# Self-attention scores in three single PSUM banks with one exponential per head, and a shared ring of four banks in place of five

## The chip, the cores and the metric

The kernel runs on one NeuronCore of one Trainium2 chip. The metric is the time of one execution on the device in microseconds (us). PE is the matrix engine, PEld its weight loads, DVE the vector engine, ACT the scalar (activation) engine, POOL is GpSimd, SP issues the DMAs. PSUM, where PE writes its results, has eight banks; a bank holds 512 float32 numbers on each of 128 partitions.

## The reference

Four layers run over `x` of shape 4 x 1024 x 256 (batch, tokens, features), all in float32:

```python
# L0: block with adaLN, rotary positions, a self mask, cross attention over 77 context tokens, MLP
x = x + g_msa * (attn(q, k, v, mask) @ attn_out_W)
x = x + g_x * (attn(qc, kc, vc) @ co_W)
x = x + g_mlp * (gelu(xm @ mlp_W1 + mlp_b1) @ mlp_W2 + mlp_b2)
# L1: prototypes, a router and three experts, gated; no self attention
# L2: the same shape of block as L0, self attention without mask or rotary positions
# L3: a second cross attention over the context
def attn(q, k, v):
    s = einsum('bhqd,bhkd->bhqk', q, k) * scale      # 16 heads of width 16
    return einsum('bhqk,bhkd->bhqd', softmax(s), v)
```

The change concerns the self attention of L0 and L2 directly, and everything else of L0, L2 and L3 through the PSUM banks. In L0 only 256 of the 1024 keys count for the inputs given (the path called `few`).

## The kernel before, in words

The program is written by engine, in the five blocks `@block.sync`, `.tensor`, `.vector`, `.scalar` and `.gpsimd`, with semaphores between them. L1 has banks of its own choice. L0 is one `Region` (`FEWR`), L2 and L3 are another (`L2R`). A region has one list of tokens, `R.order`, which a planner (`overlapped`) writes from estimated costs and due times; every engine walks the same list and does its part of each token. The planner isn't touched, so the order is the same before and after.

The tokens: `lnT` turns normalised rows (two banks), `qk` and `v` are the projections, `slot` is a piece of self attention, `oT`/`oP` the output projection, `cq`, `cm`, `cn`, `cs`, `cp`, `ct` are the six steps of cross attention, `m1`/`m2` the MLP. `cm` computes scores to find their maxima, and takes four banks at once; DVE reduces them one by one (L1564). `cn` turns the maxima into a row, which DVE adds into the queries in two updates (L1570). `cs` computes four score tiles, one bank each, which ACT exponentiates (L1743). `cp` is the product with the values, copied out by ACT (L1680), and `ct` turns the result back. For one half of a batch's queries `cross_tokens` writes `cm[0], cm[1], cm[2], cn[0], cm[3], cs[0], cn[1], cp[0], cs[1], ct[0], ...`; the planner puts tokens of other streams between them.

A slot has scores for 128 keys x 512 queries of four heads (one key tile), and beside them "fills", score tiles for a later group whose row maxima DVE takes (L1424, in L0 L1422), and the product of the slot before. PE does it in two halves:

```python
for half in range(2):
    if score is not None:
        scores(score, half)
    for key in R.fills(fills, half):
        fill(key)
    if half == 0 and product is not None:
        pv(product)
```

`scores(t, half)` makes two heads, `fill` one tile, two fills a half; the four matmuls sit in four 32-row groups of the array and run side by side. `pv(t)` makes four products into the accumulator bank 7. There are 64 slots with scores in L0 and 256 in L2; each region begins with slots that have fills alone.

The banks: 0 and 1 belong to the scores. A half writes both, one ACTIVATE (L1701) reads both, 1024 columns, into `PB` and counts `R.ex` up; the next half waits for that count. Banks 2 to 6 are the ring: every other result of a region takes the next one in turn (`take`), whoever makes it, after waiting that the reader of the key five before it has counted `ring_free` up. Bank 7 is the accumulator. All matmuls go through the helper at L814; transposes have lines of their own (L960 `oT` tails, L971, L980 `lnT`/`oT`, L1078 `cn`, L1100 `ct`). PE's instructions are issued in order, so a wait in one holds up all behind it.

Of the kernel before, what the change touches and what calls it, by code (L numbers as in the profile page):

```python
# [11 lines left out]
ACT = mybir.ActivationFunctionType  # L12
AX = mybir.AxisListType

P = 128
# [4 lines left out]
HG = 4  # L20
NG = H // HG
HALF = 512
# [39 lines left out]
def pixart_kernel(nc, io):  # L62
    ctx = ExitStack()
    with ctx:
# [183 lines left out]

        RING = (2, 3, 4, 5, 6)
        ACC = 7  # L250

        class Region:
# [3 lines left out]
            def __init__(self, name, l, few, overlap):  # L256
# [19 lines left out]
                n = 0  # L276
                for tok in self.order:
# [9 lines left out]
                    for add in self.bias_adds(tok):  # L287
                        self.adds[add] = len(self.adds)
                self.ring_full, self.ring_free = (sems(name + side, "0 1 2 3 4") for side in ("ring_full", "ring_free"))
                self.s_full, self.ex, self.pv, self.acc, self.nm, self.rec, self.crec = sems(name, "scores_T_full exp_done pv_done acc_out max_done recip cross_recip")  # L290
# [68 lines left out]
            def closing(self):  # L359

                return sorted(self.number, key=self.number.get)[-5:]

            def bank(self, key):
                return RING[self.number[key] % 5]

            def full(self, key):
                return self.ring_full[self.number[key] % 5], self.number[key] // 5 + 1

            def freed(self, key):
                return self.ring_free[self.number[key] % 5], self.number[key] // 5 + 1  # L370

            def fills_up(self, key):
                return self.ring_full[self.number[key] % 5]

            def frees(self, key):
                return self.ring_free[self.number[key] % 5]

# [434 lines left out]
        def _(pe):  # L812
# [69 lines left out]
            def region_pe(R):  # L882
                def take(key):
                    n = R.number[key]
                    if n >= 5:
                        pe.wait_ge(R.ring_free[n % 5], n // 5)
                    return RING[n % 5]

# [25 lines left out]
                def scores(t, half):  # L914
                    b, g, qh, i = R.at(t)
                    kt = R.keys[i]
                    pair = 2 * t + half
                    if pair:
                        pe.wait_ge(R.ex, pair)
                    if half == 0 and i == 0:  # L920
                        pe.wait_ge(*R.freed(("nm", b * NG + g, qh)))
                    for j in (2 * half, 2 * half + 1):
                        rows = slice(32 * j, 32 * j + 32)
                        last = mm(PS[:, j % 2, :], KE[rows, g, kt * P:(kt + 1) * P], QE[rows, g, qh * HALF:(qh + 1) * HALF], True, not R.masked)
                        if R.masked:
                            for q in range(4):
                                last = mm(PS[:, j % 2, q * P:(q + 1) * P], MQ[:, qh * 4 + q, kt * P:(kt + 1) * P], bigI[:, :], False, q == 3)
                    last.then_inc(R.s_full, 1)

                def pv(t):  # L930
                    b, g, qh, i = R.at(t)
                    pe.wait_ge(R.ex, 2 * t + 2)
                    if i == 0:
# [744 lines left out]
        def _(act):  # L1678
# [9 lines left out]
            def region_act(R):  # L1688
# [5 lines left out]
                def slot(tok):  # L1694
                    _, score, fills, product, tails, nms = tok
                    if score is not None:
                        for half in range(2):
                            act.wait_ge(R.s_full, 2 * score + half + 1)
                            if half == 0 and score >= 2:
                                act.wait_ge(R.pv, score - 1)  # L1700
                            act.activation(PB[:, score % 2, 2 * half:2 * half + 2, :], PS[:, 0:2, :], ACT.Exp, scale=SCALE).then_inc(R.ex, 1)  # L1701
                    if product is not None and (product + 1) % R.per == 0:
# [241 lines left out]
```

## Time and profile before

| | us |
|---|---|
| three runs | 3990.29, 3999.54, 3999.25 |
| median | 3999.25 |
| the profiled execution | 3986.81 |
| its span (first to last instruction) | 3985.0 |
| PE busy | 3486.6 (87%) |
| DVE busy | 1784.5 (45%) |
| ACT busy | 1386.0 (35%) |
| mean granted TensorE clock | 0.905 of full |

L0 runs to about 1170 us, L1 from there to about 1890, L2 and L3 from there to the end. Busy times are of instructions alone; two engines can be busy at once. A group's idle time is that of its engine just before its instructions, with what ended it. The end of a matmul is modelled, so bursts that follow each other overlap a little in the timeline (1.14 us long, 1.07 apart). The timeline merges instructions of one line and shape that follow each other; `x8` for float32 matmuls is four matmuls of two passes each.

### The profile page before, as it was taken

To read this page: it belongs to the slowest core of one execution; us is meant where nothing else is said; L and a number is where in the kernel's file an instruction comes from. 1 tells how busy PE (TensorE), PEld (TensorE's weight loads), DVE (VectorE), ACT (ScalarE), POOL (GpSimd) and SP (SyncE) were. 2 spreads that over 40 slices of the span, in tenths; PEclk is the share of its full clock that TensorE was granted. 3 is DMA by queue.
4 is the path that set the end of the run, shared out by engine and by line. 5 is a ranking of instruction groups with operands and counts; after the bars stand their busy time and mean duration, and the time that the engine had idled before them with its cause. 6 is when DMAs were issued, how large, how long until landed. Compare 5 with 4: busy or idle time off the path is not lost.

```text
span 3985.0 us, 49765 instructions
## 1 busy us (share of the span) xinstructions
PE 3486.6 (87%) x20728; PEld 1892.7 (47%) x20728; DVE 1784.5 (45%) x3670; ACT 1386.0 (35%) x1933; POOL 242.6 (6%) x208
## 2 busy tenths in 40 slices
PE   5789989898859898998878889998999989999887
PEld 2555756655646464655412234433445334542464
DVE  4775465433211111212766665466654565551323
ACT  0244435342311212021144435444454445444232
POOL 0100000000000000001000010000100001000010
PEclk7898989898969898999799989899899999998696
DMA  5100000000020000001000000000000000000000
GB/s 173 52 5 1 7 18 7 18 5 14 1 84 0 0 0 1 0 0 57 1 1 1 1 6 3 1 20 9 6 3 14 14 6 1 3 14 14 1 1 11
DMA packets 57344, 57.40 MB, mean 14 GB/s; under 512 B 18452, under 2 KB 51336, under 8 KB 56852
## 3 DMA queue, kind: packets, MB, share of 16 engines
q1 hardware_dynamic: 57116, 54.14, 4.3%
q8 instruction: 170, 2.79, 0.3%
q14 instruction: 58, 0.48, 0.0%
HBM read 46.24 MB, written 7.89 MB: 14 GB/s over the span
## 4 chain that ended last, share of the span: by engine, by line
PE 75%; ACT 13%; DVE 8%; issue 2%; SPq 1%; DMA 1%; POOL 0%; DVEq 0%; ACTq 0%
PE ps L814 69%; ACT big L1701 10%; PE ps L980 2%; ACT probs L1743 2%; DVE row_max_cross L1564 1%; PE ps L1100 1%; DVE max_halves L1424 1%; DVE big L1570 1%; PE ps L971 1%; ACT L1701 1%; PE ps L960 1%; DVE bn_stats L1476 0%; DVE xn_tok L1489 0%; DMA big<-in_L_xcond_bss_kv 0%; DVE bn_stats L1455 0%
## 5 line engine op out<-in xcount | busy, mean ns | idle before, releaser
L1701 ACT ACTIVATE big<-ps 128x1024 f32<-128x1024 f32 x640 | 655.9, 1025 | 1035.7 <-PE ps L814 1034.6
L814 PE MATMUL ps<-big 32*128 32x512 f32 (+1 forms) x5632 | 864.7, 636 | 153.8 <-ACT big L1701 116.3
L1424 DVE TENSOR_REDUCE max_halves<-ps 128x1 f32<-128x512 f32 x1024 | 655.3, 686 | 453.4 <-PE ps L814 452.4
L814 PEld LDWEIGHTS ps<-big 32*128 32x128 f32 x5632 | 323.8, 195 | 638.8 <-ACT big L1701 515.3
L814 PE MATMUL ps<-big,probs 128*32 128x512 f32 x2560 | 365.0, 644 | 0.0
L814 PE MATMUL ps<-weights_mlp,big 128*128 128x256 f32 (+1 forms) x1088 | 243.4, 380 | 6.9 <-ACT big L1680 4.4
L814 PE MATMUL ps<-k_v_cross,big 32*128 32x77 f32 x3072 | 146.4, 342 | 112.5 <-DVE row_max_cross L1564 63.4
L814 PE MATMUL ps<-x_T,weights_mlp 128*128 128x256 f32 x1024 | 232.9, 386 | 3.0 <-ACT x_T L1718 3.0
L1743 ACT ACTIVATE probs<-ps 77x512 f32<-77x512 f32 x384 | 197.3, 592 | 96.4 <-PE ps L814 96.3
L1461 DVE TENSOR_TENSOR x_tok<-ps,x_tok 128x512 f32<-128x512 f32 x112 | 77.5, 692 | 342.2 <-PE ps L814 342.0
L814 PEld LDWEIGHTS ps<-weights_mlp,big 128*128 128x128 f32 (+1 forms) x1088 | 207.6, 199 | 43.9 <-issue 11.6
L814 PE MATMUL ps<-x_T,probs 128*128 128x512 f32 x448 | 217.1, 607 | 5.2 <-DVE o_T L1647 5.2
L814 PEld LDWEIGHTS ps<-x_T,weights_mlp 128*128 128x128 f32 x1024 | 196.4, 194 | 37.6 <-issue 5.6
L1564 DVE TENSOR_REDUCE row_max_cross<-ps 128x4 f32<-128x308 f32 x384 | 156.9, 472 | 123.8 <-PE ps L814 123.8
L1422 DVE TENSOR_REDUCE row_max<-ps 128x2 f32<-128x512 f32 x256 | 163.2, 686 | 100.6 <-PE ps L814 100.2
L814 PE MATMUL ps<-weights,x_T 128*128 128x256 f32 x768 | 199.3, 409 | 4.7 <-ACT x_T L1680 2.5
L814 PE MATMUL ps<-weights,big 128*128 128x256 f32 x896 | 203.2, 383 | 0.0
L814 PEld LDWEIGHTS ps<-k_v_cross,big 32*128 32x128 f32 x3072 | 131.8, 246 | 142.5 <-issue 102.1
L814 PE MATMUL ps<-big,k_v_cross 32*77 32x512 f32 x768 | 177.0, 706 | 10.4 <-DVE big L1570 7.1
L814 PEld LDWEIGHTS ps<-weights,big 128*128 128x128 f32 x896 | 167.5, 190 | 35.6 <-issue 14.5
L814 PEld LDWEIGHTS ps<-weights,x_T 128*128 128x128 f32 x768 | 149.8, 203 | 60.6 <-issue 33.4
L1877 POOL TENSOR_SCALAR eps_tile<-mean_var 128x4 f32<-128x4 f32 x56 | 13.5, 241 | 2666.1 <-DVE mean_var L1482 2666.1
(217 smaller groups left out, 3284.2 us busy)
## 6 DMA issues: line engine op xcount, KB each, us to landing
weights_mlp<-in_L_xcond_mlp_W SPq DMA_DIRECT2D x5, 1024.0 KB, 5.4
weights_mlp<-in_L_xcond_W_mlp SPq DMA_DIRECT2D x5, 1024.0 KB, 5.3
x_tok<-in_x SPq DMA_DIRECT2D x4, 1024.0 KB, 9.8
out_y<-x_tok SPq DMA_DIRECT2D x8, 512.0 KB, 2.9
probs<-in_L_xcond_e_w SPq DMA_DIRECT2D x3, 1024.0 KB
gates_biases<-mod_rows SPq DMA_DIRECT2D x20, 128.0 KB, 5.1
big<-in_L_xcond_adaLN_W SPq DMA_DIRECT2D x1, 2304.0 KB
kc_groups<-big SPq DMA_DIRECT2D x3, 616.0 KB, 4.0
```

The lines of the kernel that those rows point to most:

```text
L814: return pe.matmul(out, lhsT, rhs, start=first, stop=last)
L960: last = pe.transpose(PS[:, bank, i * P:(i + 1) * P], OT[:, c:c + P], ident[:, :])
L971: last = pe.transpose(PS[:, bank, i * P:(i + 1) * P], NM[:, gg % 2, qt:qt + P], ident[:, :])
L980: last = pe.transpose(PS[:, banks[ft], (t % 4) * P:(t % 4 + 1) * P], rows[:, t, ft * P:(ft + 1) * P], ident[:, :])
L1100: last = pe.transpose(PS[:, bank, i * P:(i + 1) * P], OTC[:, i * P:(i + 1) * P], ident[:, :])
L1422: dve.tensor_reduce(NM[:, e, c:c + 2], PS[:, bank, :].rearrange("p (t n) -> p t n", t=2), AX.X, ALU.max, negate=True).then_inc(R.frees(key ...
L1424: dve.tensor_reduce(NMP[:, e, j, s // NH, s % NH:s % NH + 1], PS[:, bank, :], AX.X, ALU.max, negate=True).then_inc(R.frees(key), 1)
L1461: dve.tensor_tensor(x, PS[:, R.bank(key), :], x, ALU.add).then_inc(R.frees(key), 1)
L1564: dve.tensor_reduce(NMC[:, hf, g // 2, c:c + 4], src, AX.X, ALU.max, negate=True).then_inc(R.frees(key), 1)
L1570: last = dve.scalar_tensor_tensor(q, PS[:, R.bank(tok), :], maxrow(e), q, ALU.mult, ALU.add)
L1701: act.activation(PB[:, score % 2, 2 * half:2 * half + 2, :], PS[:, 0:2, :], ACT.Exp, scale=SCALE).then_inc(R.ex, 1)
L1743: act.activation(PC[0:NC, j, :], PS[0:NC, R.bank(key), :], ACT.Exp, scale=SCALE).then_inc(R.frees(key), 1)
```

## The change

Head `n` of the scores (counted through all slots of a region) goes to bank `n % 3` of three, PE waits before each head for the exponential of head `n - 3`, every head counts `R.s_full` up, and ACT runs one ACTIVATE of 512 columns per head instead of one of 1024 per pair. The product waits for all four exponentials of its slot, as before. The ring loses bank 2 and turns over banks 3 to 6. The whole diff:

```diff
--- before.py
+++ after.py
@@ -246,7 +246,8 @@
 
             return ap.rearrange("p (t n) -> p t n", n=288)[:, :, 0:272].rearrange("p t (h c) -> p t h c", c=17)[:, :, :, HD:HD + 1]
 
-        RING = (2, 3, 4, 5, 6)
+        SCORES = (0, 1, 2)
+        RING = (3, 4, 5, 6)
         ACC = 7
 
         class Region:
@@ -286,7 +287,7 @@
                         self.loads[tok[1:]] = sum(1 for k in self.loads if k[0] == tok[1])
                     for add in self.bias_adds(tok):
                         self.adds[add] = len(self.adds)
-                self.ring_full, self.ring_free = (sems(name + side, "0 1 2 3 4") for side in ("ring_full", "ring_free"))
+                self.ring_full, self.ring_free = (sems(name + side, "0 1 2 3") for side in ("ring_full", "ring_free"))
                 self.s_full, self.ex, self.pv, self.acc, self.nm, self.rec, self.crec = sems(name, "scores_T_full exp_done pv_done acc_out max_done recip cross_recip")
                 self.ln_st, self.ln_mv, self.ln_ep, self.ln_rs, self.ln_norm = sems(name + "ln_", "stats mean_var eps rstd rows")
                 self.rp_f, self.qe, self.ke = sems(name, "turned groups_act groups_dve")
@@ -358,22 +359,22 @@
 
             def closing(self):
 
-                return sorted(self.number, key=self.number.get)[-5:]
+                return sorted(self.number, key=self.number.get)[-4:]
 
             def bank(self, key):
-                return RING[self.number[key] % 5]
+                return RING[self.number[key] % 4]
 
             def full(self, key):
-                return self.ring_full[self.number[key] % 5], self.number[key] // 5 + 1
+                return self.ring_full[self.number[key] % 4], self.number[key] // 4 + 1
 
             def freed(self, key):
-                return self.ring_free[self.number[key] % 5], self.number[key] // 5 + 1
+                return self.ring_free[self.number[key] % 4], self.number[key] // 4 + 1
 
             def fills_up(self, key):
-                return self.ring_full[self.number[key] % 5]
+                return self.ring_full[self.number[key] % 4]
 
             def frees(self, key):
-                return self.ring_free[self.number[key] % 5]
+                return self.ring_free[self.number[key] % 4]
 
             def qk_steps(self, b, m):
                 return [("qk", b, m, a, hf) for a in range(2) for hf in range(1 if a and self.few else NH)]
@@ -882,9 +883,9 @@
             def region_pe(R):
                 def take(key):
                     n = R.number[key]
-                    if n >= 5:
-                        pe.wait_ge(R.ring_free[n % 5], n // 5)
-                    return RING[n % 5]
+                    if n >= 4:
+                        pe.wait_ge(R.ring_free[n % 4], n // 4)
+                    return RING[n % 4]
 
                 def done(last, key):
                     last.then_inc(R.fills_up(key), 1)
@@ -914,22 +915,21 @@
                 def scores(t, half):
                     b, g, qh, i = R.at(t)
                     kt = R.keys[i]
-                    pair = 2 * t + half
-                    if pair:
-                        pe.wait_ge(R.ex, pair)
                     if half == 0 and i == 0:
                         pe.wait_ge(*R.freed(("nm", b * NG + g, qh)))
                     for j in (2 * half, 2 * half + 1):
-                        rows = slice(32 * j, 32 * j + 32)
-                        last = mm(PS[:, j % 2, :], KE[rows, g, kt * P:(kt + 1) * P], QE[rows, g, qh * HALF:(qh + 1) * HALF], True, not R.masked)
+                        rows, n = slice(32 * j, 32 * j + 32), 4 * t + j
+                        if n >= 3:
+                            pe.wait_ge(R.ex, n - 2)
+                        last = mm(PS[:, SCORES[n % 3], :], KE[rows, g, kt * P:(kt + 1) * P], QE[rows, g, qh * HALF:(qh + 1) * HALF], True, not R.masked)
                         if R.masked:
                             for q in range(4):
-                                last = mm(PS[:, j % 2, q * P:(q + 1) * P], MQ[:, qh * 4 + q, kt * P:(kt + 1) * P], bigI[:, :], False, q == 3)
-                    last.then_inc(R.s_full, 1)
+                                last = mm(PS[:, SCORES[n % 3], q * P:(q + 1) * P], MQ[:, qh * 4 + q, kt * P:(kt + 1) * P], bigI[:, :], False, q == 3)
+                        last.then_inc(R.s_full, 1)
 
                 def pv(t):
                     b, g, qh, i = R.at(t)
-                    pe.wait_ge(R.ex, 2 * t + 2)
+                    pe.wait_ge(R.ex, 4 * t + 4)
                     if i == 0:
                         if t:
                             pe.wait_ge(R.acc, t // R.per)
@@ -1694,11 +1694,12 @@
                 def slot(tok):
                     _, score, fills, product, tails, nms = tok
                     if score is not None:
-                        for half in range(2):
-                            act.wait_ge(R.s_full, 2 * score + half + 1)
-                            if half == 0 and score >= 2:
+                        for j in range(HG):
+                            n = 4 * score + j
+                            act.wait_ge(R.s_full, n + 1)
+                            if j == 0 and score >= 2:
                                 act.wait_ge(R.pv, score - 1)
-                            act.activation(PB[:, score % 2, 2 * half:2 * half + 2, :], PS[:, 0:2, :], ACT.Exp, scale=SCALE).then_inc(R.ex, 1)
+                            act.activation(PB[:, score % 2, j, :], PS[:, SCORES[n % 3], :], ACT.Exp, scale=SCALE).then_inc(R.ex, 1)
                     if product is not None and (product + 1) % R.per == 0:
                         q = product // R.per
                         act.wait_ge(R.pv, product + 1)
```

## Rows read from the trace of the kernel before

**Rows 1.** The page: span, busy time, chain by engine and by line.

```profile
span 3985.0 us, 49765 instructions
...
PE 3486.6 (87%) x20728; PEld 1892.7 (47%) x20728; DVE 1784.5 (45%) x3670; ACT 1386.0 (35%) x1933; POOL 242.6 (6%) x208
...
PE 75%; ACT 13%; DVE 8%; issue 2%; SPq 1%; DMA 1%; POOL 0%; DVEq 0%; ACTq 0%
PE ps L814 69%; ACT big L1701 10%; PE ps L980 2%; ACT probs L1743 2%; DVE row_max_cross L1564 1%; PE ps L1100 1%; DVE max_halves L1424 1%; DVE big L1570 1%; PE ps L971 1%; ACT L1701 1%; PE ps L960 1%; DVE bn_stats L1476 0%; DVE xn_tok L1489 0%; DMA big<-in_L_xcond_bss_kv 0%; DVE bn_stats L1455 0%
```

**Rows 2.** Groups of the whole span: shapes, count | busy us, mean ns | idle, releaser.

```profile
L1701 ACT ACTIVATE big<-ps 128x1024 f32<-128x1024 f32 x640 | 655.9, 1025 | 1035.7 <-PE ps L814 1034.6
L1424 DVE TENSOR_REDUCE max_halves<-ps 128x1 f32<-128x512 f32 x1024 | 655.3, 686 | 453.4 <-PE ps L814 452.4
...
L1743 ACT ACTIVATE probs<-ps 77x512 f32<-77x512 f32 x384 | 197.3, 592 | 96.4 <-PE ps L814 96.3
```

**Rows 3.** What PE waited for, whole span: us in total, times, longest us.

```profile
PE ps L814 <- ACT big L1701: 116.3, 133, 1.2
PE ps L814 <- DVE row_max_cross L1564: 63.4, 44, 3.3
```

**Rows 4.** The same view, 1960 to 2260 us.

```profile
PE ps L814 <- ACT big L1701: 56.9, 55, 1.1
```

**Rows 5.** Timeline of one dense slot: start us, duration us, what [idle before].

```profile
3192.83 1.14 PE L814 MATMUL ps<-big 32*128 32x512 f32 x8 [1.11 <-ACT big L1701]
...
3193.90 1.06 PE L814 MATMUL ps<-big,probs 128*32 128x512 f32 x8
3194.00 1.03 ACT L1701 ACTIVATE big<-ps 128x1024 f32<-128x1024 f32 x1 [1.23 <-PE ps L814]
...
3195.08 1.14 PE L814 MATMUL ps<-big 32*128 32x512 f32 x8
3196.25 1.02 ACT L1701 ACTIVATE big<-ps 128x1024 f32<-128x1024 f32 x1 [1.23 <-PE ps L814]
...
3197.33 1.14 PE L814 MATMUL ps<-big 32*128 32x512 f32 x8 [1.11 <-ACT big L1701]
```

**Rows 6.** Timeline around a cm behind a cn.

```profile
2377.01 0.66 PE L1078 MATMUL ps<-ident,row_max_cross 128*128 128x128 f32 x4
...
2378.37 1.40 DVE L1570 SCALAR_TENSOR_TENSOR big<-ps,group_cols,big 128x512 f32<-128x512 f32 x2
...
2378.60 1.13 PE L814 MATMUL ps<-k_v_cross,big 32*128 32x77 f32 x32 [0.93 <-DVE max_halves L1424]
```

**Rows 7.** Timeline, cm behind cm.

```profile
2753.05 1.64 DVE L1564 TENSOR_REDUCE row_max_cross<-ps 128x4 f32<-128x308 f32 x4 [0.67 <-PE ps L814]
...
2754.44 1.13 PE L814 MATMUL ps<-k_v_cross,big 32*128 32x77 f32 x32 [1.38 <-DVE row_max_cross L1564]
```

**Rows 8.** Timeline, cs behind cp.

```profile
3154.72 0.21 PEld L814 LDWEIGHTS ps<-big,k_v_cross 32*77 32x77 f32 x2 [0.27 <-DVE max_halves L1424]
3154.73 0.60 ACT L1680 ACTIVATE o_T_cross<-ps 128x512 f32<-128x512 f32 x1
```

**Rows 9.** Timeline, cs behind a slot.

```profile
2594.32 1.29 DVE L1424 TENSOR_REDUCE max_halves<-ps 128x1 f32<-128x512 f32 x2 [0.96 <-PE ps L814]
2595.07 0.21 PEld L814 LDWEIGHTS ps<-big,k_v_cross 32*77 32x77 f32 x2 [0.84 <-DVE max_halves L1424]
```

**Rows 10.** Timeline, a slot behind cs and ct.

```profile
3155.34 2.05 ACT L1743 ACTIVATE probs<-ps 77x512 f32<-77x512 f32 x4
...
3156.31 1.28 PE L814 MATMUL ps<-big 32*128 32x512 f32 x8
```

**Rows 11.** Stretches: us, busy of PE, PEld, DVE, ACT, POOL, granted clock, DMA share, GB/s.

```profile
1960.00:2260.00 300.00, 236.03 (x1664) 68.87 (x1664) 184.66 (x306) 137.02 (x140) 3.62 (x3) 0.99 0.00 1
2260.00:3700.00 1440.00, 1319.68 (x8926) 604.22 (x8920) 780.79 (x1523) 651.19 (x848) 104.99 (x77) 0.93 0.03 8
...
2752.00:2760.00 8.00, 5.23 (x103) 4.66 (x104) 4.70 (x12) 0.07 (x1) 0.00 (x0) 0.72 0.01 2
```


## The prediction

> **What bounds the kernel now.** The page first: PE is busy 87% of the span, ACT 35%, DVE 45%, and the chain that ended last runs 75% through PE and 13% through ACT, of which the score exponential of L1701 is most [rows 1]. So the kernel is PE-bound, with one partner that PE waits for. The groups say how much of that partner there is: 640 exponentials of 1.025 us, with 1035.7 us of idle ACT time before them, nearly all of it spent waiting for PE [rows 2]. ACT is far from full. It is the hand-over that costs: two banks are written, read by one exponential, and only then written again. PE's own waits give the size: 116.3 us in 133 waits are ended by L1701, the longest 1.2 us; DVE's cross-attention maxima end another 63.4 us in 44 [rows 3]. Nearly half of the first sum, 56.9 us in 55 waits, lies in the 300 us from 1960 to 2260, where slots follow each other with nothing between [rows 4].
>
> The timeline of one such slot shows the pattern [rows 5]. Scores and fills start at 3192.83, the products at 3193.90 (1.07 later), the second scores only at 3195.08 (1.18 later, 0.11 of it waiting), because the exponential ran from 3194.00 to 3195.03. The second exponential runs 3196.25 to 3197.27 and the next slot starts at 3197.33, 2.25 after the second scores although the burst itself takes 1.07. A slot is 4.50 us for 3 x 1.07 = 3.21 us of PE work. Where other work stands between two slots, the 1.18 us is already filled and only the 0.11 inside is lost.
>
> **The change, the gain side.** Head n needs the exponential of head n-3. The two heads of a burst take two of the three banks, so only one is ahead. Call U the start of the second burst of a slot (heads 2 and 3). Today's exponentials start 1.17 after their burst (3192.83 to 3194.00, 3195.08 to 3196.25) and PE goes on 0.05 after their end [rows 5]; so head 2's exponential starts at U+1.17. A 512-column exponential is not in the trace on 128 partitions, the nearest is L1743 with 0.592 us [rows 2]; it ends at U+1.76. Head 0 of the next slot starts at U+1.07 without waiting (its bank was freed before), head 1 needs head 2's bank and starts at U+1.81. The fills stand behind head 1 on PE's queue, then the products, so the next second burst is at U+1.81+2x1.07 = U+3.95. Head 3 of it needs the exponential of its own slot's head 0, long done. A dense slot thus goes from 4.50 to 3.95 us: 0.55 is won of the 1.29 that wait today. Bounds: 1.29 if the third bank hid everything, and minus 0.32 if the hand-over stayed serial (4 x 0.592 against 2 x 1.025 us). Half of the 116.3 us is 57 us. The 0.11 us inside a slot goes entirely, since head 3 waits for one exponential that ended 0.4 us earlier; counted along the trace it is there in some 240 of the 320 scored slots, of which [rows 5] is one: 26 us. Together **83 us** won.
>
> ACT gets 640 more instructions. Four exponentials of L1743 in a row take 2.05 us [rows 10], as long as two of today's 1.02; apart they cost 2 x 0.592 - 1.025 = 0.16 us a pair, 102 us in all, inside 1035.7 us of idle time. I charge nothing; with ACT in the way it would be up to 102. The 640 more semaphore increments and waits on PE are not visible in any row; nothing, or up to 0.05 us on one in ten, 3 us.
>
> The Trainium skill, "ScalarE: Activation LUTs", section on what ACT_TABLE_LOAD costs, speaks against splitting: every ACTIVATE has a fixed part of 186 ns, 93 ns of which overlap when they follow back to back. That would be 640 x 0.093 = 60 us if ACT were on the path. The row of four in 2.05 us is shorter than four times its single time, which agrees with the overlap.
>
> **The change, the cost side.** Everything else on PE (fills, tails, projections, cross attention, MLP) passes through the ring, now of four banks. A token that takes n banks must wait for the reader of the key four back, not five. PE's queue is in order, so each such wait is PE's. By neighbours in the order the planner writes (counted from its code, which the change doesn't alter):
> - cm takes all four banks, so it waits for the key just before it. After cn that is the update of L1570: cm started at 2378.60, the two updates end at 2379.77, with 0.06 for the hand-over 1.23 us more [rows 6]. 26 such places: 32 us.
> - cm after cm: today it starts when three of the four maxima are out, at 2754.44; the fourth ends at 2754.69 [rows 7], 0.30 more. 42 places: 13 us.
> - cs: its fourth bank is now that of the key before it. After cp (64 of the 96) this is read by the copy of L1680, which ends at 3155.33 where the fourth score was loaded at 3154.72 [rows 8]: 0.66 there, nothing where that copy is early; I take 0.35: 22 us. After a slot (25) it is the last fill's maximum: the pair ends at 2595.61, the fourth score was loaded at 2595.07 [rows 9], 0.59: 15 us.
> - The first fills of a slot that follows ct, cs, lnT or cm (88 slots): the second fill, in the burst at 3156.31, needs the third of four exponentials that run from 3155.34, done at 3156.91, and not the second, done at 3156.42 (spaced by (2.05 - 0.59) / 3 = 0.49) [rows 10]: 0.49 there, nothing where other work intervened; I take 0.25: 22 us.
> - Single takes (ct, cn, oT, oP, lnT, qk, some 150 that stand close behind their reader): between 0 and 0.6, I take 0.3: 45 us.
>
> That is 149 us of new waits, each taken alone. They are not wholly additive. A late cs does not matter at the region's ends (24 of 96), where PE waits for its exponentials anyway, and a wait of PE lets DVE work off what the next wait would have been for. I take off a quarter: **115 us** lost; bounds 50 us (mostly hidden) and 195 us (nothing hidden, the zeros above rarely so).
>
> Other engines: DVE needs 4 x 0.686 = 2.74 us a slot [rows 2], under 3.95, so it does not become the bound in dense slots. No DMA is moved; SP's waits are on the same keys and have their margin.
>
> **The sum.** -83 + 115 = +32 us. The profiled execution took 3986.81 us (span 3985.0) and would go to about 4019. The three runs had a median of 3999.25, 12.4 above it; the same difference on the median gives **4031 us**, 0.8% slower.
>
> **Rivals.**
> 1. The rotation wins and the ring is hidden (the other sign). The mixed stretch has waits of its own that may swallow the new ones: then 83 won (up to 142, the 116.3 and the 26 whole) against 50 lost: 3999 - 83 + 50 = 3966. For it: DVE and ACT are each under half busy [rows 1]. Against: the 63.4 us for L1564 [rows 3] are ring waits already, with five banks. The Trainium skill, "Perfetto Trace Analysis", Matmuls, says that independent groups should rotate through banks so that evacuation overlaps the next group; by it alone the time falls. It doesn't say that the banks come from another rotation. Chance 0.24.
> 2. The two sides cancel, within 0.3% (12 us, about what a measurement here can tell): gain 83 against 71 to 95. 0.15.
> 3. The ring waits count in full and pull the clock down. In 2752 to 2760, a run of cm with PE idle 1.4 us before each [rows 7], the mean granted clock is 0.72, so part of it was at 1.2 GHz; in the dense stretch it is 0.99, all but wholly 2.4 GHz; in the 1440 us of mixed work 0.93 [rows 11]. With 195 us lost and one per cent of those 1440 us more for the clock (14 us), 3999 - 83 + 195 + 14 = 4125. 0.20.
> 4. My forecast, 4011 to 4075: 0.41.
>
> The change does what it says: the pairs are single in code on both sides, so no rival there. Rival 1 decides once the ring costs under 71 us, half of the new waits taken alone.
>
> So faster 0.24, same 0.15, slower 0.61. The range is 3965 to 4125; the forecast's own is 4011 to 4075.
>
> **What would show it.** Right: exponentials x1280 of about 0.59 us; in 1960 to 2260 the dense slots at 3.95 us, with PE waiting some 0.7 us for L1701 within the first burst; PE's waits for L1564, L1424, L1570 and L1743 together up by about 100 us. Wrong on the gain: dense slots at 3.2 or at 4.5. Wrong on the ring: cm after cn starts less than 1 us after where it did, or these waits rise by under 50 us. A mean clock below 0.89 would speak for rival 3.

## The result, and the profile after

The changed kernel took 4106.61 us (median of four runs, 4102.14 to 4107.59) against 3997.16 us for the kernel before, run beside it: a ratio of 1.0275, with 1.0257 to 1.0292 as its 95% interval. It is some 110 us slower. The prediction had the sign and the range right (3965 to 4125), and its number, 4031, was 76 us short. The profiled execution took 4105.83 us, 119 us more than that of before.

The page of the changed kernel, to be held against [rows 1]:

```profile
span 4104.0 us, 50404 instructions
...
PE 3662.4 (89%) x20728; PEld 2001.6 (49%) x20728; DVE 1789.6 (44%) x3670; ACT 1428.2 (35%) x2573; POOL 242.0 (6%) x208
...
PE 87%; DVE 9%; ACT 1%; issue 1%; SPq 1%; DMA 1%; POOL 0%; DVEq 0%; ACTq 0%
```

ACT has gone from 13% of the chain to 1%. What the change was about is done, and the kernel is slower. PE executes the same 20,728 matmuls, and is "busy" for 176 us longer: 89% busy here is not better than 87% before. The mean granted clock fell from 0.905 to 0.884.

The groups of the changed kernel (busy us, mean ns | idle before, releaser; the helper of L814 is now L815, the exponential of L1701 is L1702):

```profile
L1702 ACT ACTIVATE big<-ps 128x512 f32<-128x512 f32 x1280 | 695.7, 596 | 979.6 <-PE ps L815 978.9
L815 PE MATMUL ps<-big 32*128 32x512 f32 (+1 forms) x5632 | 959.3, 640 | 16.5 <-ACT big L1702 5.5
...
L815 PE MATMUL ps<-k_v_cross,big 32*128 32x77 f32 x3072 | 167.4, 378 | 170.9 <-DVE row_max_cross L1564 75.8
```

Scores and fills, cs scores (x768) and cm scores (x3072) in the kernel before, whose exponentials stand in [rows 2]:

```profile
L814 PE MATMUL ps<-big 32*128 32x512 f32 (+1 forms) x5632 | 864.7, 636 | 153.8 <-ACT big L1701 116.3 <-DVE row_max L1422 4.9 <-DVE max_halves L1424 4.0
...
L814 PE MATMUL ps<-big,k_v_cross 32*77 32x512 f32 x768 | 177.0, 706 | 10.4 <-DVE big L1570 7.1 <-DVE xn_tok L1414 3.3
...
L814 PE MATMUL ps<-k_v_cross,big 32*128 32x77 f32 x3072 | 146.4, 342 | 112.5 <-DVE row_max_cross L1564 63.4 <-DVE max_halves L1424 19.6 <-ACT probs L1743 18.7
```

The scores and fills (x5632) lost 137 us of idle time and took 95 us more of busy time. That is partly bookkeeping: a wait between head 0 and head 1 lies inside a burst, where the profile still counts PE as busy. So the two columns are read as a sum: 1018.5 before, 975.8 after, 43 us gained. The cm scores (x3072) lost 79 us, by the same sum.

What PE waited for, against [rows 3]; the exponential of L1702 is no longer among the waits of note:

```profile
PE ps L815 <- DVE row_max_cross L1564: 84.8, 57, 3.3
PE ps L815 <- DVE big L1570: 57.4, 27, 3.5
```

L1570 is the update of the queries behind cn. In the kernel before:

```profile
PE ps L814 <- DVE big L1570: 8.7, 9, 1.9
```

The timeline of a dense slot of the changed kernel, to be held against [rows 5]:

```profile
2093.24 2.94 PE L815 MATMUL ps<-big 32*128 32x512 f32 x16
...
2094.21 0.18 PEld L815 LDWEIGHTS ps<-big 32*128 32x128 f32 x1 [0.24 <-issue]
2094.39 1.08 ACT L1702 ACTIVATE big<-ps 128x512 f32<-128x512 f32 x2 [1.46 <-PE ps L815]
...
2095.04 0.31 PEld L815 LDWEIGHTS ps<-big 32*128 32x128 f32 x6 [0.64 <-ACT big L1702]
...
2096.11 1.07 PE L815 MATMUL ps<-big,probs 128*32 128x512 f32 x8
...
2097.10 0.31 PEld L815 LDWEIGHTS ps<-big 32*128 32x128 f32 x8 [0.84 <-ACT big L1702]
```

The second burst starts at 2093.24. Head 0 of the next slot is loaded alone at 2094.21, head 1 and the fills at 2095.04, which is U+1.80 (forecast U+1.81). The next second burst is at 2097.10: 3.86 us a slot, forecast 3.95, before 4.50. It is a typical one: of the 56 slots that follow another slot directly and have no transposes of their own, the median is 4.50 us before and 3.87 after. The PE row of 2.94 us is one row although PE stood still for part of it; the weight loads show the gap.

The timeline of the changed kernel at the place of [rows 6], a cm behind a cn:

```profile
2421.24 0.66 PE L1078 MATMUL ps<-ident,row_max_cross 128*128 128x128 f32 x4
...
2422.63 1.40 DVE L1570 SCALAR_TENSOR_TENSOR big<-ps,group_cols,big 128x512 f32<-128x512 f32 x2
...
2424.18 2.01 PE L815 MATMUL ps<-k_v_cross,big 32*128 32x77 f32 x32 [2.27 <-DVE big L1570]
...
2426.80 1.09 PE L1100 MATMUL ps<-ident,o_T_cross 128*128 128x128 f32 x4 [0.61 <-DVE row_max_cross L1564]
2427.82 0.52 PEld L815 LDWEIGHTS ps<-big 32*128 32x128 f32 x8 [0.33 <-issue]
2427.82 1.24 PE L815 MATMUL ps<-big 32*128 32x512 f32 x4
```

What followed it in the kernel before:

```profile
2379.92 0.63 PE L1100 MATMUL ps<-ident,o_T_cross 128*128 128x128 f32 x4 [0.19 <-DVE big L1570]
2380.47 1.28 PE L814 MATMUL ps<-big 32*128 32x512 f32 x8
```

From cn to the next slot PE took 3.46 us before (2377.01 to 2380.47) and 6.58 after (2421.24 to 2427.82): 3.1 us more, where the forecast charged 1.23. The wait itself is close to the forecast: cm starts 2.94 after cn in place of 1.59, 1.35 more. Then the same cm matmuls take 2.01 us in place of 1.13, and the transposes of ct 1.09 in place of 0.63, together 1.35 more again. The last 0.4 us is a second ring wait: ct now waits 0.61 us for the first maximum of cm (L1564), where 0.19 stood before. The stretches show the clock (columns as in [rows 11]); first the changed kernel, then the one before:

```profile
2421.00:2428.10 7.10, 4.21 (x48) 3.25 (x48) 4.42 (x9) 1.08 (x2) 0.00 (x0) 0.69 0.00 0
```

```profile
2377.00:2380.70 3.70, 2.58 (x48) 2.08 (x47) 3.54 (x7) 1.02 (x1) 0.00 (x0) 1.00 0.00 0
```

The granted clock is 1.00 (2.4 GHz throughout) before, and 0.69 after, so partly 1.2 GHz. It was 1.00 from 2421 to 2423 and 0.50 from 2424 to 2430, so it fell within the idle 2.27 us, and behind them the same matmuls took up to 1.8 times as long. Here the wait is paid a second time in the work that follows. This place is worse than most, as the list below shows, and the kernel before has low stretches too (0.57 from 2374 to 2377); over the whole span the mean went from 0.905 to 0.884.

To see the whole, each token of PE's order was charged with the time from the last matmul of the token before it to its own last matmul, in both traces. After minus before: slots -78 us (those in L2 -69, in L0 -9), cm +78, cs +48, ct +16, lnT +13, lead-in slots with fills alone +9, oP +9, m1 +7, cq, cn, cp and m2 +15 together. These sum to +117, the 119 us between the spans but for rounding. By neighbour: cm after cn, 26 places, +40 us or 1.5 each (forecast 1.23); cm after cm, 42 places, +22 (forecast 13); cs after cp, 64 places, +31 (forecast 22); cs after a slot, 25 places, +15 (forecast 15). New to the list: cm after a slot, 13 places, +10, and ct after cm, 16 places, +13.

### The profile page after: what moved, and what is told of

Same layout as the page of the kernel before. It is cut to its first block, busy times and chain, and to the rows that moved or that the text cites. A ratio compares the mean times of both kernels' runs of the same rounds, so it can differ in the third digit from the quotient of the medians.

```text
span 4104.0 us, 50404 instructions
## 1 busy us (share of the span) xinstructions
PE 3662.4 (89%) x20728; PEld 2001.6 (49%) x20728; DVE 1789.6 (44%) x3670; ACT 1428.2 (35%) x2573; POOL 242.0 (6%) x208
## 4 chain that ended last, share of the span: by engine, by line
PE 87%; DVE 9%; ACT 1%; issue 1%; SPq 1%; DMA 1%; POOL 0%; DVEq 0%; ACTq 0%
PE ps L815 79%; PE ps L980 3%; DVE row_max_cross L1564 2%; PE ps L1100 1%; DVE big L1570 1%; PE ps L971 1%; PE ps L960 1%; DVE max_halves L1424 1%; PE ps L1078 1%; ACT probs L1744 0%; DVE bn_stats L1476 0%; DVE xn_tok L1489 0%; DVE bn_stats L1455 0%; DMA big<-in_L_xcond_bss_kv 0%; PE ps L1153 0%
## 5 line engine op out<-in xcount | busy, mean ns | idle before, releaser
L1702 ACT ACTIVATE big<-ps 128x512 f32<-128x512 f32 x1280 | 695.7, 596 | 979.6 <-PE ps L815 978.9
L815 PE MATMUL ps<-big 32*128 32x512 f32 (+1 forms) x5632 | 959.3, 640 | 16.5 <-ACT big L1702 5.5
L1424 DVE TENSOR_REDUCE max_halves<-ps 128x1 f32<-128x512 f32 x1024 | 655.8, 685 | 444.6 <-PE ps L815 442.5
L815 PEld LDWEIGHTS ps<-big 32*128 32x128 f32 x5632 | 380.2, 197 | 515.2 <-ACT big L1702 316.4
L815 PE MATMUL ps<-big,probs 128*32 128x512 f32 x2560 | 362.2, 639 | 0.0
L815 PE MATMUL ps<-k_v_cross,big 32*128 32x77 f32 x3072 | 167.4, 378 | 170.9 <-DVE row_max_cross L1564 75.8
L815 PE MATMUL ps<-weights_mlp,big 128*128 128x256 f32 (+1 forms) x1088 | 244.1, 381 | 7.6 <-ACT big L1680 4.4
L815 PEld LDWEIGHTS ps<-k_v_cross,big 32*128 32x128 f32 x3072 | 151.5, 280 | 202.2 <-issue 154.9
L1564 DVE TENSOR_REDUCE row_max_cross<-ps 128x4 f32<-128x308 f32 x384 | 156.9, 471 | 200.6 <-PE ps L815 200.6
L815 PE MATMUL ps<-x_T,weights_mlp 128*128 128x256 f32 x1024 | 238.8, 393 | 3.3 <-ACT x_T L1719 1.9
L815 PE MATMUL ps<-big,k_v_cross 32*77 32x512 f32 x768 | 227.3, 732 | 7.8 <-DVE xn_tok L1414 3.3
L815 PEld LDWEIGHTS ps<-weights_mlp,big 128*128 128x128 f32 (+1 forms) x1088 | 207.9, 200 | 46.8 <-issue 13.3
L815 PE MATMUL ps<-x_T,probs 128*128 128x512 f32 x448 | 218.2, 609 | 5.2 <-DVE o_T L1647 5.2
L815 PEld LDWEIGHTS ps<-x_T,weights_mlp 128*128 128x128 f32 x1024 | 200.5, 198 | 40.2 <-issue 8.0
L815 PE MATMUL ps<-weights,x_T 128*128 128x256 f32 x768 | 206.5, 420 | 5.5 <-DVE row_max_cross L1564 3.0
L815 PE MATMUL ps<-weights,big 128*128 128x256 f32 x896 | 203.2, 383 | 0.0
L815 PEld LDWEIGHTS ps<-weights,x_T 128*128 128x128 f32 x768 | 154.6, 209 | 63.7 <-issue 35.5
L815 PEld LDWEIGHTS ps<-weights,big 128*128 128x128 f32 x896 | 167.5, 190 | 35.6 <-issue 14.5
```

The costliest lines, as they stand in the source:

```text
L815: return pe.matmul(out, lhsT, rhs, start=first, stop=last)
L1424: dve.tensor_reduce(NMP[:, e, j, s // NH, s % NH:s % NH + 1], PS[:, bank, :], AX.X, ALU.max, negate=True).then_inc(R.frees(key), 1)
L1564: dve.tensor_reduce(NMC[:, hf, g // 2, c:c + 4], src, AX.X, ALU.max, negate=True).then_inc(R.frees(key), 1)
L1702: act.activation(PB[:, score % 2, j, :], PS[:, SCORES[n % 3], :], ACT.Exp, scale=SCALE).then_inc(R.ex, 1)
```

## The experiments

**One side alone: the shorter ring.** Theory A: the ring's fifth bank is worth about 186 us, and the third score bank wins some 80 of it back. Theory B: the ring costs the 115 us of the forecast, and the rotation wins little or nothing, because a burst that a wait splits loses its side-by-side matmuls. The kernel before, its scores in pairs as they were, with bank 2 left unused:

```diff
-        RING = (2, 3, 4, 5, 6)
+        RING = (3, 4, 5, 6)
...
-                    if n >= 5:
-                        pe.wait_ge(R.ring_free[n % 5], n // 5)
+                    if n >= 4:
+                        pe.wait_ge(R.ring_free[n % 4], n // 4)
```

> The kernel before with the ring of four banks alone: pairs of heads in banks 0 and 1 with one exponential per pair as before, bank 2 left unused. Theory A (the ring's new waits count nearly in full, about 186 us, and the rotation wins about 78 us in the slots): 3997 + 186 = about 4180 us, 4160 to 4200. Rival B (the ring costs the 115 us of the forecast, and the rotation wins little or nothing because a burst that is split by a wait loses its side-by-side matmuls): about 4110 us, 4095 to 4130.

Measured: 4216.46 us, ratio 1.0562 (1.0544 to 1.0581), +223 us. The fifth bank was worth more than either theory said, above even the forecast's upper bound of 195. And the rotation of three on top of it, with its split exponentials, is worth 110 us (4216 to 4107), not 83. The page:

```profile
span 4213.2 us, 49764 instructions
...
PE 3643.0 (86%) x20728; PEld 1968.2 (47%) x20728; DVE 1792.0 (43%) x3670; ACT 1389.8 (33%) x1933; POOL 242.7 (6%) x208
```

PE's waits of this kernel:

```profile
PE ps L814 <- ACT big L1701: 113.2, 120, 1.2
PE ps L814 <- DVE row_max_cross L1564: 84.4, 57, 3.1
PE ps L814 <- DVE big L1570: 56.8, 27, 3.5
```

Its groups:

```profile
L814 PE MATMUL ps<-big 32*128 32x512 f32 (+1 forms) x5632 | 914.5, 650 | 146.9 <-ACT big L1701 113.2 <-DVE row_max L1422 4.3 <-DVE max_halves L1424 4.0
...
L814 PE MATMUL ps<-big,k_v_cross 32*77 32x512 f32 x768 | 225.1, 725 | 7.6 <-DVE xn_tok L1414 3.3 <-DVE row_max_cross L1564 1.7 <-DVE big L1570 1.4
```

The waits on L1564 and L1570 rose by 69 us, but the span by 228. Of that, 156 us is PE busy time (3486.6 to 3643.0) with the same matmuls. cs (x768) is the plainest case: busy 225.1 where it was 177.0, idle 7.6 where it was 10.4. The mean time of one of its matmuls rose from 706 to 725 ns, 3%, and the busy time by 27%, so slower matmuls are the small part of it. The weight loads of one cs of this kernel, and of one of the kernel before:

```profile
2722.16 0.51 PEld L814 LDWEIGHTS ps<-big,k_v_cross 32*77 32x77 f32 x4 [0.17 <-issue]
2723.07 0.21 PEld L814 LDWEIGHTS ps<-big,k_v_cross 32*77 32x77 f32 x2 [0.39 <-DVE max_halves L1424]
2723.69 0.14 PEld L814 LDWEIGHTS ps<-big,k_v_cross 32*77 32x77 f32 x1 [0.41 <-DVE probs L1414]
```

```profile
3154.22 0.22 PEld L814 LDWEIGHTS ps<-big,k_v_cross 32*77 32x77 f32 x6 [0.84 <-issue]
```

With four banks, two tiles start together, the third 0.9 us after them and the fourth 1.5. In the kernel before, three tiles started together at 3154.22 and the fourth at 3154.72 [rows 8]. The four row groups no longer run side by side, and since another tile is mostly still under way, the time is counted as busy. The list of waits doesn't show it.

An estimate for the whole of the 228 us: 72 are idle time. Each group's busy time multiplied by the rise of its mean ns, summed over all shapes of PE, gives another 72 for slower matmuls (mean clock 0.880 in place of 0.905). The remaining 85 or so are then matmuls that no longer run side by side.

**The other side alone: heads singly in two banks.** Five ring banks as before, each head with its own exponential, alternating between banks 0 and 1:

```diff
-                    pair = 2 * t + half
-                    if pair:
-                        pe.wait_ge(R.ex, pair)
...
+                        if n >= 2:
+                            pe.wait_ge(R.ex, n - 1)
+                        last = mm(PS[:, SCORES[n % 2], :], ...)
```

> The kernel before with the ring of five, and heads one by one: one exponential per head, head n in bank n % 2, waiting for the exponential of head n - 2. Theory A (splitting by itself is nearly free; what wins in the change is the third bank): in a dense slot the second head is free at U + 2.30 us against 2.25 for a pair, so 3997 plus 0 to 25 us, 3990 to 4025. Rival B (split bursts cost by themselves): the same loss here as in the changed kernel, 40 to 80 us, so 4037 to 4077.

Measured: 3978.71 us, 0.9975 (0.9955 to 0.9995), some 10 to 15 us better than before: neither case. Splitting costs nothing, and wins a little; the interval ends just under 1. Its dense slot:

```profile
2086.36 1.14 PE L815 MATMUL ps<-big 32*128 32x512 f32 x8
...
2088.17 1.62 PE L815 MATMUL ps<-big 32*128 32x512 f32 x8 [0.67 <-ACT big L1702]
2088.66 0.31 PEld L815 LDWEIGHTS ps<-big 32*128 32x128 f32 x6 [0.20 <-ACT big L1702]
...
2089.72 1.06 PE L815 MATMUL ps<-big,probs 128*32 128x512 f32 x8
...
2090.72 0.71 PE L815 MATMUL ps<-big 32*128 32x512 f32 x4
```

Second burst to second burst is 4.36 us (2086.36 to 2090.72) against 4.50: the burst behind the products starts 1.00 after them and not 1.18 as in [rows 5]. Head 1 is let go at 2088.66, U+2.30. In the changed kernel that was U+1.80, so the third bank's own part is the half microsecond between.

**The order around cn.** The costliest new wait is that of cm for the reader of cn. Swapping the two tokens puts cn behind the last cm, where its reader has the time of cm to finish:

```diff
-            ... cm[0], cm[1], cm[2], cn[0], cm[3], cs[0], cn[1], cp[0],
+            ... cm[0], cm[1], cm[2], cm[3], cn[0], cs[0], cn[1], cp[0],
```

Once in the changed kernel, once in the kernel before.

> The changed kernel with one swap in the list of a cross attention half: the fourth cm stands ahead of the first cn, so that no cm follows a cn. Theory A (each cm behind a cn lost 1.5 us, 26 places, against about 0.5 us for a cm behind a cm): 4107 - 26 = about 4080 us, 4065 to 4090. Rival B (the wait only moves to the next token that wants a bank, ct or a slot's fills): under 10 us, 4097 to 4112.

> The kernel before with the same swap. With five banks a cm behind a cn does not wait for the cn, so theory A expects nothing to be won: 3990 to 4010 us, and perhaps a loss of up to 10 us, since the fourth cm now waits for the third one's maxima where it had the cn between. Rival B: also no change.

Measured: 4059.47 us (1.0166, 1.0149 to 1.0183) for the changed kernel with the swap, 47 us less than without; 3986.81 us (0.9985, 0.9975 to 0.9995) for the kernel before with it, about 7 us less. Both are below what was expected. About what cm after cn had lost (40 us) comes back, or somewhat more. PE's waits in the changed kernel with the swap:

```profile
PE ps L815 <- DVE row_max_cross L1564: 120.2, 71, 3.3
...
PE ps L815 <- DVE big L1570: 14.7, 7, 3.4
```

The two together went from 142 to 135 us, so 40 of the 47 us are not in these waits: PE busy time fell by 36 us (to 3626.9), with the clock at 0.889 in place of 0.884. The wait mostly moved from L1570 to L1564: of the 26 cm behind a cn 2 are left, and 65 in place of 42 stand behind another cm. The same estimate as above, from each group's mean ns, gives 35 us less for faster matmuls (cs 695 ns in place of 732, scores and fills 633 in place of 640), so nearly all of the fall in busy time goes with the clock; that was not tried by itself.

**Which tokens pay for the fifth bank.** With five banks in place, one kind of token at a time was made to wait for the key four before it as well, as it would with four banks:

```diff
+                self.nth = sorted(self.number, key=self.number.get)
...
+                    if key[0] == "cm" and n >= 4:
+                        pe.wait_ge(*R.freed(R.nth[n - 4]))
```

with `"cm"` in the first, `"cs"` in the second, and `not in ("cm", "cs")` in the third.

> The kernel before, all five ring banks in use, but each cm also waits for the reader of the key four back, as a ring of four would make it. Theory A (the ring of four costs through these waits alone, and the kinds add up: by token against before, the ring of four gave 69 us to cm, 46 to cs, 108 to all others): 3990 + 69 = about 4060 us, 4045 to 4080. Rival C (the waits overlap: one takes the place of another, as the forecast's quarter supposed): cm alone costs more than its share, 90 us or more.

> The same with cs alone. Theory A: 3990 + 46 = about 4036 us, 4020 to 4050. Rival C: 60 us or more.

> The same with every key but those of cm and cs. Theory A: 3990 + 108 = about 4098 us, 4075 to 4115; much of it would be time that cm and cs hand on. Rival C: more than 125 us. If on the contrary the others cost less than 60 us alone, the rest of the ring's cost belongs to what a late cm or cs does to the tokens behind it, and the sum of the three falls short of the 223 us of the whole ring.

Measured, over the 3990.44 us of the kernel before beside them: cm 4071.72 us (1.0197, 1.0172 to 1.0222), +81; cs 4037.51 us (1.0120, 1.0096 to 1.0144), +47; the rest 4126.16 us (1.0341, 1.0318 to 1.0365), +136. cs and cm lie inside A's ranges, cm near the upper end; the rest lies above A's and past C's mark of 125. The sum is 264 us, against 223 for the ring of four: an overlap of 15% or so, if these added nothing but the wait meant. They may: each adds a wait instruction of its own to every token concerned, and in the third that is every fill. The scores and fills of the third:

```profile
L815 PE MATMUL ps<-big 32*128 32x512 f32 (+1 forms) x5632 | 971.5, 639 | 123.9 <-ACT big L1704 99.6 <-DVE row_max L1425 4.3 <-DVE max_halves L1427 4.0
```

They are busy for 971.5 us, and in the kernel with the ring of four for 914.5; busy and idle together it is 1095 against 1061. The share of the rest lies between 95 us (223 less 81 and 47) and 136; where, stays open, but 34 of the 41 us between these bounds are in this one group.

The second of these runs also settles what happened to cs, since only its waits were added (lines stand three further down here):

```profile
L815 PE MATMUL ps<-big,k_v_cross 32*77 32x512 f32 x768 | 231.6, 711 | 14.5 <-DVE row_max_cross L1567 6.8 <-DVE xn_tok L1417 3.8 <-DVE big L1573 1.5
```

The mean matmul takes 711 ns against 706, and the group is busy for 231.6 us against 177.0. The 55 us are no longer running four wide, and not the clock. For cm it is the other way: with its waits alone its idle time rose by 65 us (112.5 to 177.2) and its busy time by 11.

**A third bank without the price.** If the third bank pays in dense stretches and the fifth in mixed ones, bank 2 can be lent. Theory A: nearly all of the dense gain, and no ring loss. Theory B: turning the bank over costs what it wins. The heads are single; while the order is written, a run of at least `LEND` slots with nothing between takes bank 2 out of the ring and gives it back at its end:

```diff
+                        if inside and 0 in ring:
+                            ring.remove(0)
+                            mine.append(RING[0])
...
+                        elif not inside and 0 not in ring:
+                            mine.remove(RING[0])
+                            ring.append(0)
```

The first head in the lent bank waits for the ring key that had it, the first ring key after for the last exponential of it. First with `LEND = 3`; beside it, in the same set of runs, the split heads alone with the cm and cn swap, and lending with the swap.

> Heads one by one as in the kernel with two single score banks, and bank 2 lent: in runs of three or more slots with nothing between them the scores rotate through banks 0, 1 and 2 and the ring through 3 to 6; everywhere else the scores have banks 0 and 1 and the ring has 2 to 6. Theory A (the third score bank is worth something only where slots follow each other, 62 + 9 us in the changed kernel, and the fifth ring bank only where they don't): the two-bank kernel's 3979 us less what it leaves there, 71 - 24 = 47 us, plus a few for the hand-overs: about 3935 us, 3920 to 3950. Rival B (the slots of a dense run need the fifth ring bank too, or the hand-overs between runs cost what is won): 3965 to 3995.

> Two single score banks, ring of five, and the fourth cm ahead of the first cn. If the two effects are independent: 3979 - 7 = about 3972 us, 3962 to 3982.

> The lent bank and the swap of cm and cn together. Theory A: the lent bank's time less 7 us, about 3928 us, 3910 to 3945. Rival B: no better than 3960.

Measured, against 3983.37 us of the kernel before in that set: lending 3923.02 us (0.9842, 0.9824 to 0.9860), in A's range; heads in two banks with the swap 3975.72 us (0.9985, 0.9976 to 0.9994), in its range; lending with the swap 3913.81 us (0.9832, 0.9819 to 0.9846), in A's range. The first and the last intervals overlap, and the second's ratio is no better than the 0.9975 without the swap: with five banks the swap is worth nothing that these runs can tell. The lent bank takes 1.3% off the split heads (0.9842 against 0.9975), some 53 us, with no ring loss: the rotation's dense gain by itself. The stretch of [rows 4] under lending:

```profile
1960.00:2260.00 300.00, 298.99 (x1836) 107.04 (x1836) 206.12 (x342) 157.50 (x288) 3.61 (x3) 0.99 0.00 1
```

1,836 matmuls in the 300 us in which the kernel before did 1,664 [rows 11].

**How short a run is worth lending to.** Lending with the swap, with `LEND` at 2 and at 1 in place of 3:

> The lent bank with the swap, lending already in runs of two slots and not only of three. A run of two has one place where a slot follows a slot, worth about 0.5 us, against two hand-overs of bank 2. Theory A: within 8 us of the kernel that lends from three on (3914 us on its chip, ratio 0.983): ratio 0.981 to 0.985.

> The same lending in every slot, also where a single slot stands between tokens of other kinds. Theory A (away from the dense runs the fifth ring bank is worth more than the third score bank): each of the single slots now pays at its borders, so 20 to 60 us slower than lending from three on: ratio 0.988 to 1.0. Rival B (lending is free wherever it is done): ratio below 0.983.

Measured: with 2, 3908.96 us (0.9797, 0.9779 to 0.9815), the lowest time of all and a little under what was expected, 2.0% under the kernel before and 198 us under the changed one; with 1, 3928.83 us (0.9845, 0.9824 to 0.9865), between its two cases and 20 us slower than with 2. Whether 2 is better than 3 is not shown: the order has only three runs of exactly two slots, the single times of both kernels overlap (3903 to 3915 and 3907 to 3923 us), and the ratios differ mainly because the kernel before took 3994 us beside one and 3983 beside the other. The loss with 1 is clear: 214 slots stand alone. That such a slot gains less from a third score bank than it and its neighbours lose by a ring of four and by the hand-overs is the likely reading; which of the two it is, wasn't tried. The page of the kernel with 2:

```profile
span 3901.4 us, 50416 instructions
...
PE 3510.1 (90%) x20728; PEld 1953.2 (50%) x20728; DVE 1788.6 (46%) x3670; ACT 1425.8 (37%) x2573; POOL 242.6 (6%) x208
```

Its granted clock is 0.915, above the 0.905 of before, and PE's busy time is 152 us under that of the changed kernel for the same matmuls.

## Why the prediction was right in sign and short in size

**What bounds.** Right. PE is the bound in both, and ACT's exponentials were the partner it waited for; with them gone the chain is 87% PE and 1% ACT.

**The gain side, 83 us.** Right in mechanism, and somewhat small. Dense slots take 3.86 us (forecast 3.95), head 1 is let go at U+1.80 (forecast 1.81), the 116.3 us of waits on L1701 fell to 5.5 (what is left of them lies inside bursts and counts as busy), and the slots as a whole won 78 us, with the first fills' loss already in that. Beside the short ring alone the rotation won 110, 27 more than the term; some 10 to 15 of that is the split itself, which had been given nothing. Lent, and with no ring loss, the third bank won some 53 beyond the split, against the 57 taken for half of the waits.

**ACT at nothing.** Right. 1,280 exponentials of 0.596 us, 42 us more of ACT's time, and 980 us of its idle time left; the split alone came out 0.25% faster. The Trainium skill, "ScalarE: Activation LUTs", on what ACT_TABLE_LOAD costs, gives an estimate of 60 us with ACT on the path; two exponentials back to back took 1.08 us here against 1.03 for one of 1024 columns, 0.05 more where the page's figures give 0.09, and that lay beside PE's work.

**The ring, 115 us.** This is the step that failed, the size of the ring's term. Its mechanism was right: a token waits for the reader of the key four back, cm after cn most of all. The cost was 223 us by the shorter ring alone, or 117 + 78 = 195 in the changed kernel by the tokens other than scored slots. By neighbours as the prediction put them: cm 32 + 13 = 45 forecast, 81 with cm's waits alone; cs 22 + 15 = 37, 47 alone; singles 45 and first fills 22, together 67, and 95 to 136 for all the rest. By token it can be told apart. The single takes were priced well: they lost 44 us in the changed kernel and 50 with the ring of four alone, where 45 stood. cm and cs lost 126 and 115 us, where 82 stood. The lead-in slots, cq, cp, m1 and m2 lost 26 and 30 us, where nothing stood. The slots with scores lost 32 us with the ring of four alone, where 22 stood for the first fills. Of overlap some 34 us were taken off (149 to 115); the three runs show 15% or so of what was measured alone, 22 us of 149, so that choice cost about 12 us. With nothing taken off, 149 would still have been 74 short of 223. The prices of cm and cs and the tokens without a term were the larger miss, not the overlap. In the sum the two errors partly cancel: the gain was 27 us too small, the loss 108.

**Why the prices were small.** Each was the length of one wait, read from when the last reader ends. Two things come on top, both seen above. The burst behind the wait is slower when the clock has fallen (2.01 us for 1.13, clock 0.69 in that stretch), and a burst of four whose last tile is late no longer runs four wide (cs busy 231.6 for 177.0 with its waits alone). For cs the second is shown. For the whole there is only the estimate above, some 72 us for the first and 85 for the second in the ring of four alone; no run holds the clock fixed. The prediction read the first in [rows 7, 11] (clock 0.72 in a run of cm), but put it into rival 3 alone, at 14 us for the mixed work, and not into each price.

**The rivals.** Rival 3, ring waits in full with the clock pulled down, gave 4125 at a chance of 0.20 and came nearest; its own sign, a mean clock below 0.89, is there (0.884). Its terms, 83 won and 209 lost, were both too small (110 and 223), and the two errors offset each other. Rival 1, the ring hidden behind DVE and ACT at under half busy, fell: the waits are of single readers in order, and an engine at 45% is no help to a wait for its next instruction. By the Trainium skill, "Perfetto Trace Analysis", Matmuls, independent groups should rotate through banks; the runs agree for the bank by itself (0.9842 against 0.9975) and disagree for it as paid by the other rotation (1.0275).

**What would show it.** "PE's waits for L1564, L1424, L1570 and L1743 up by about 100 us" was a poor sign. In the matmuls of the helper they rose by 53 us, from 118 to 171 (L1564 and L1570 by 70, the other two fell by 17), just above the 50 that would have spoken against the ring's cost. Most of the loss stands in PE's busy time, where no list of waits shows it.

## What to carry to other kernels

PSUM banks are one stock: before taking one from a rotation, take it away alone and see what it was worth there, for here the fifth ring bank was worth 223 us and the third score bank, with split exponentials, 110. Where the two are needed in different stretches, lend it by a rule fixed while the order is written (1.6 to 2.0% faster than before). Price a new wait on PE as the wait, plus the following bursts at the lower clock, plus the four-wide bursts that it breaks, and compare busy plus idle time of a group, since a wait inside a burst counts as busy. With a short rotation, put a result with a slow reader ahead of work that doesn't need all the banks: moving one token was worth 47 us with four banks, and little with five.

## What was not expected of the hardware

- The same 20,728 matmuls kept PE busy for 3486.6, 3662.4, 3643.0 and 3510.1 us in the kernel before, the changed one, the ring of four and the one that lends from runs of two on. The mean granted clocks were 0.905, 0.884, 0.880 and 0.915.
- Splitting one ACTIVATE of 1024 columns (1.025 us) into two of 512 in separate banks cost no time on the path and won 0.25%; the burst behind the products starts 1.00 us after them in place of 1.18.
- Where only the waits of cs were added, its 768 matmuls kept PE busy for 231.6 us in place of 177.0, while the mean of one stayed at 711 ns against 706: the fourth of four tiles came late.
- A PE idle time of 2.27 us came before a stretch at a clock of 0.69, in which cm took 1.8 times as long (2.01 for 1.13 us) and the transposes 1.7 times (1.09 for 0.63).
